# Second expert layer of two steps put together behind every even step of the first layer (steps 2 to 28)

## The reference

```python
h = x @ Wm + bm
t = h.reshape(bs * L_ * H, HD)              # 8 heads of 32 per token
logits = t @ expert_emb
w = jax.nn.softmax(logits, axis=-1)
topw, topi = jax.lax.top_k(w, K)            # K = 2 of 16 experts
hmid = jax.nn.gelu(jnp.einsum('td,edi->tei', t, W1) + b1, approximate=False)
eo = jnp.einsum('tei,eio->teo', hmid, W2) + b2
sel = jnp.take_along_axis(eo, topi[:, :, None], axis=1)
comb = (sel * topw[:, :, None]).sum(axis=1)
out = comb.reshape(bs, L_, d) @ Wo + bo
```

## Time and profile before

| | us |
|---|---|
| time, median of 3 runs | 3078.34 |
| lowest and highest | 3070.01, 3086.05 |
| the profiled execution, its own time | 3081.99 |
| its span, first to last instruction | 3080.3 |
| TensorE busy | 2900.5 |
| VectorE busy | 1912.2 |
| ScalarE busy | 1801.5 |
| GpSimd busy | 1326.3 |

### The profile page before, as it was taken

How to read it: one execution, slowest core, us unless ns; L and a number is a source line. 1 busy time by engine, 2 the same in 40 slices (tenths; PEclk the granted TensorE clock), 3 DMA queues, 4 the chain that set the end, 5 groups by cost and what they waited for, 6 DMA issues and landing times.

```text
span 3080.3 us, 51536 instructions
## 1 busy us (share of the span) xinstructions
PE 2900.5 (94%) x16460; PEld 1262.3 (41%) x16460; DVE 1912.2 (62%) x4637; ACT 1801.5 (58%) x2146; POOL 1326.3 (43%) x1355
## 2 busy tenths in 40 slices
PE   5689999999998999989999999999999999999999
PEld 2234444444444444444444444444444444444433
DVE  5465656757657566675666756666666657667453
ACT  1244675456754667546674466745676556754586
POOL 3312465135552365513644146542465225652254
PEclk7789999999999999999999999999999999999999
DMA  6101453024530344303442044420453113530242
GB/s 143 37 25 27 122 135 89 26 59 108 137 92 3 87 110 127 73 1 100 114 117 67 1 119 113 108 57 16 126 128 92 38 48 107 141 82 20 66 127 89
DMA packets 176245, 252.54 MB, mean 82 GB/s; under 512 B 50797, under 2 KB 82557, under 8 KB 175885
## 3 DMA queue, kind: packets, MB, share of 16 engines
q1 hardware_dynamic: 168988, 247.26, 31.0%
q10 hardware_dynamic: 6996, 1.99, 0.3%
HBM read 159.13 MB, written 12.63 MB: 56 GB/s over the span
## 4 chain that ended last, share of the span: by engine, by line
PE 84%; DVE 8%; issue 3%; ACT 1%; SPq 1%; DMA 0%; POOL 0%; POOLq 0%; ACTq 0%; DVEq 0%
PE ps L1248 17%; PE ps L1211 16%; PE ps L1266 16%; PE ps L1232 8%; PE ps L412 7%; PE ps L458 4%; PE ps L510 2%; PE ps L499 2%; PE ps L529 2%; PE ps L460 2%; DVE front L555 2%; PE ps L486 1%; PE ps L517 1%; PE ps L444 1%; PE ps L468 1%
## 5 line engine op out<-in xcount | busy, mean ns | idle before, releaser
L1330 ACT ACTIVATE rest<-ps 128x1024 f32<-128x1024 f32 x1024 | 993.1, 1022 | 372.8 <-PE ps L1248 370.2
L1312 ACT ACTIVATE rest<-ps 128x1024 f32<-128x1024 f32 (+3 forms) x768 | 607.4, 811 | 686.4 <-PE ps L1211 675.2
L1417 POOL TENSOR_TENSOR rest<-rest 128x512 f32<-128x512 f32 x480 | 630.6, 1314 | 654.2 <-DVE rest L1366 647.7
L552 DVE CUSTOM_DVE_ANT_0 rest<-ps,maskd 128x128 f32<-128x128 f32 (+3 forms) x1024 | 461.0, 488 | 283.9 <-PE ps L412 277.3
L1248 PE MATMUL ps<-wide,w1s 98*128 98x512 f32 x2048 | 624.5, 425 | 10.8 <-ACT rest L1330 10.8
L1407 POOL TENSOR_SCALAR_AFFINE_SELECT rest<-rest 128x256 f32<-128x256 f32 x512 | 216.6, 432 | 901.5 <-ACT rest L1312 875.6
L1266 PE MATMUL ps<-rest,w2s 128*32 128x512 f32 x4096 | 548.2, 607 | 0.6 <-ACT rest L1330 0.6
L1366 DVE SCALAR_TENSOR_TENSOR rest<-ps,b2c,wide 128x512 f32<-128x512 f32 x512 | 382.7, 747 | 266.0 <-PE ps L1266 240.5
L1248 PEld LDWEIGHTS ps<-wide,w1s 98*128 98x128 f32 x2048 | 339.3, 188 | 495.3 <-ACT rest L1330 355.4
L1211 PE MATMUL ps<-wide 49*128 49x512 f32 (+3 forms) x2304 | 498.6, 526 | 2.9 <-DMA wide<-front 2.9
L555 DVE TENSOR_REDUCE front<-ps 128x1 f32<-128x512 f32 x512 | 329.6, 685 | 163.6 <-PE ps L412 157.6
(11 more groups left out here) (136 smaller groups left out, 2328.6 us busy)
## 6 DMA issues: line engine op xcount, KB each, us to landing
wide<-gate_rows SPq DMA_DIRECT2D x1024, 128.0 KB, 2.8
wide<-front SPq DMA_DIRECT2D x480, 64.0 KB, 2.0
wide<-front SPq DMA_DIRECT2D x192, 128.0 KB, 2.3
ao<-in_x SPq DMA_DIRECT2D x16, 512.0 KB, 5.3
heads<-front SPq DMA_DIRECT2D x64, 128.0 KB, 2.4
xs<-in_x SPq DMA_DIRECT2D x16, 512.0 KB, 4.7
out<-xs SPq DMA_DIRECT2D x16, 512.0 KB, 3.5
wide<-ao SPq DMA_DIRECT2D x96, 64.0 KB, 2.3
```

The costliest lines, as they stand in the source:

```text
L552: v.tensor_tensor_reduce(out=R.junk[hh][:, 0:w], in0=src[:, 0:w], in1=L.maskd[:, HALF - w:], scale=1.0, scalar=-3e38, op0=ALU.add, op1=ALU ...
L1312: nc.scalar.activation(L.pt[:, u % PTS, :, f:HALF], L.ps[:, 2 * (u % 2):2 * (u % 2) + 2, 0:HALF - f], ACT.Exp, scale=SCALE).then_inc(S["c_ ...
L1330: nc.scalar.activation(L.hm[:, u % HM, :], bank(2 * (u % 2), 2), ACT.Gelu).then_inc(S["e_gelu"], 1)
L1417: g.tensor_tensor(dst, dst, L.gy[:, k % GY, :], ALU.add).then_inc(S["e_add"], 1)
```

## The change

For q from 2 to 28 the two outers `outer(q - 2)` and `outer(q - 1)` stand one behind the other in each even step, behind `inner(2q + 1)` and in front of the items of step q. Odd steps up to 27 have no outer, and step 1 has none. From step 29 on the order is the old one. VectorE follows in the same order: `gated(q - 2)` and `gated(q - 1)` in front of the items of an even step. ScalarE, GpSimd and SP keep their programs, and so do all the waits.

```diff
+TWOS = 28
...
+def outers_behind(q):
+
+
+    return (q - 2, q - 1) if 0 < q <= TWOS and q % 2 == 0 else ()
...
                     if q == 0:
                         values(img, NM - 1)
+                    for done in outers_behind(q):
+                        outer(img, done)
                     for item in eslots[img][q]:
                         item_matmuls(pe, L, RE[img], item)
-                    if q:
+                    if q > TWOS:
                         outer(img, q - 1)
...
                 for q in range(NQ):
+                    for done in outers_behind(q):
+                        gated(done)
                     for item in eslots[img][q]:
                         item_vector(v, L, RE[img], item)
-                    if q:
+                    if q > TWOS:
                         gated(q - 1)
```

## The result

The changed kernel took 3109.3 us in the median of 8 runs (3094.31 to 3118.77), the kernel before 3080.94 (3070.01 to 3094.46): ratio 1.0087, interval 1.0063 to 1.0111. Compared again later it was 1.0063 (1.0040 to 1.0086). So it is slower by 0.6 to 0.9%, on the side of 0.5% that the prediction held a little more likely, and by more than the 3092 it gave. Its upper end was 3108: the median lies just beyond, and by the ratio on the 3078.3 from which the prediction counted the time is 3105. The profiled execution took 3114.32 us, its span is 3112.6, 32.3 more than before.

A forecast was written before the change was run, and what follows sets the result against it. TensorE, busy 94% of the span, was taken as the bound. Images 0 to 6 -1.0, image 7 +12.6 and new clock falls 2.6 made 14 us: 3092 us against the median 3078.3, own range 3082 to 3096, 8 in 10 3079 to 3108.

The forecast's parts named there:

- The price of a pair without items: Two steps without items take 5.63 us against 4.43, +1.20 per pair, as the gelu waits for its buffer's outer.
- Steps 1 to 9: Images 0 to 6: step 1 to step 9 takes 25.36 us against 22.43, +2.9.
- clock term: Three new falls of TensorE's clock in all, 2.6 us; bounds 0 and fifteen falls, 13 us.
- the recurrence: Step starts worked out from which gelu or outer each instruction waits for; 5.63 us per pair without items.
- Steps 9 to 15: Idle before L510 shrinks from 1.47 to 0.35, no fall; step 15 0.6 earlier in images 0 to 4, 1.0 later in 5, 6.
- Steps 15 to 29: Images 0 to 6: 51.05 us against 51.03, switches saved and short waits before steps 19, 23 and 26 cancelling.
- The saving at the switches: Inner following a full-array item avoids switch costs; bounds 0 and 0.3 us per pair, taken near 0.3.
- rival 3: Slower: item then inner saves nothing, some 20 switches in 7 images lose 0.1 each; 8 us more, 3100 us; 22%.
- the sum of images 0 to 6: Change up to step 29: five images 0.6 us earlier, two 1.0 later, together -1.0 us.
- Image 7: Last image, without items to hide late gelus: +12.6 us up to step 29, reaching 94 us.
- rival 2: Slower: late gelus chop TensorE's work, ten to fifteen clock falls at 0.87 instead of three; 3102 us; 23%.
- Rival 1: Faster: the switches decide, each of 112 pairs saving 0.3, 34 us, with gelu lateness absorbed in images 0 to 6; 3049 us; 7%.

The follow-up runs named there:

- the run with six buffers: The changed kernel with six instead of four gelu buffers in the last image; one time, 3072.5 us.
- the repeats: Score matmuls of two attention slots repeated with the same operands: on the kernel before 3061.31 us (0.9934), on the changed kernel 3076.07 us (0.9988).
- second profile: The changed kernel again with no edit; median 3101.8 us, ratio 1.0063 to the kernel before.

## Why the prediction was right on the side and short on the size

**The price of a pair without items**: 5.63 worked out, 5.70 measured. The wait from the outer's start to the gelu was 1.20, not 1.13: `gated` started 1.14 behind the same outer, ScalarE ran one instruction of its wait first. The time of the step was right, its reason only partly: I laid the price on the buffer of the gelu, and the run with six buffers shows that most of it would be there without.

**Steps 1 to 9**: step 9 at 27.7 forecast, 27.75 found, step by step within 0.3 (8.55, 15.95, 22.08 for steps 3, 5, 7 against the 8.61, 16.21, 22.10 of the recurrence). In images 3 to 5 the clock fell once in these steps, +0.6: the "new falls" of the clock term. The prediction took image 6 for one without a fall, like image 5. It had no fall in step 10, but one in step 1 (105.81 us in all), and the changed kernel had one in step 2 of it (106.40).

**Steps 9 to 15**: right in kind. The idle time in front of L510 is gone altogether (0.35 forecast), the fall of the clock with it. L449 began 0.1 earlier and not 0.4 later (49.97 for 50.08 behind step 0), without the 1.59 of idle time that it had in front of it. Step 15 began 1.6 earlier than before in images 0 to 4, where I had 0.6; 0.3 of this is only that the record puts the first matmul of an inner earlier when it follows a full-array item (the second comes 0.64 behind it and not 0.34).

**Steps 15 to 29**: 51.87 for 51.03 against my 51.05 (51.57 without that 0.3). These two errors cancel: step 29 began at 105.13, forecast 105.3, and that it came so near is luck. The saving at the switches was taken rightly near its upper bound: the last matmul of L510 starts at 720.20 and the second of the inner behind it at 720.87, 0.43 + 0.24, so a full-array item then inner costs nothing, and rival 3 falls. The rule of the Trainium skill, "TensorEngine Tiling (Array Packing)", section Key Properties, that a change of the tiling mode drains TensorE, is borne out for the changes from or to the four column tiles of an outer, and the inner behind an item of 64 rows or 64 columns (`v`, `kc`, `std`) pays the 0.34 too; between a full-array item and an inner there is no such change, and no cost. Outer then full-array item costs 0.52 to the item's start, as I had carried over, but its first matmul of 512 columns takes 0.53 and not 0.43 (0.65 and 0.51 in front of L510), about 0.1 more in a pair.

**Steps 29 to 62**: here a term was left out. I closed the sum of images 0 to 6 at the *start* of step 29. The gelus of step 28 are late there, so step 29 takes 2.83 for 2.37 and nothing behind it gives the 0.47 back: 3.3 us over seven images, of the 3.6 of all eight. In image 7 I had counted it (0.3).

**Image 7**: +12.6 forecast, +13.7 found in the first profile, and +15.7 between the two kernels with the repeats (94.23 for 78.50), of which the slower has lower clock in two places and the faster in none. The mechanism was right: steps 17 to 28 took 36.7, which is the 34.2 of the sum and 2.5 for two falls. The table loads were nearly right: steps 15 and 16 took 10.2 for 8.6, 1.6 more where I had 1.3, with TensorE idle 3.55 in front of step 16 (the first line below) for 2.55. That the total is so near is luck again, as two things which the sum didn't hold nearly cancel. The kernel before had a fall in step 1 of this image (4.61 us for 3.04, the first window below), the changed one had not: step 9 began 1.4 later and not 2.9. And the changed one had the two falls, in the pairs without items at steps 20 and 28 (the other two windows, 5.05 and 5.12 for 3.85).

```profile
2976.54 2.14 PE L1255 MATMUL ps<-wide,w1s 98*128 98x512 f32 x4 [3.55 <-ACT rest L1339]
```
```profile
2906.91:2911.52 4.61, 4.43 (x17) 1.70 (x17) 0.68 (x2) 3.18 (x4) 0.50 (x1) 0.63 1.01 231
```
```profile
2989.08:2994.13 5.05, 4.87 (x21) 1.22 (x21) 2.86 (x5) 1.95 (x3) 1.84 (x2) 0.66 0.36 104
3013.07:3018.19 5.12, 4.92 (x20) 1.30 (x21) 0.75 (x1) 1.94 (x3) 0.86 (x2) 0.67 0.30 86
```

**The clock**: three new falls at 0.87 in the expert stages. Found in the first profile: one in steps 1 and 2 of each of images 3, 4 and 5, and two in image 7, against five gone at step 10 and one in step 1 of image 7. With 3 x 0.6 and 2 x 1.2 this is 4.2 for my 2.6, inside the bounds of the term, and rival 2 (ten to fifteen) falls. Pieces of 0.2 us rarely did it, but they did: in the pair of steps ahead of both falls of image 7 TensorE idled only 0.18 to 0.34 at a time. What the term missed is the attention stage. I had read its spread only as the 16 us between three runs and left it at "about what can't be told from no change". It is a cost that the kernel before carries in a certain amount, 3.7 us in five of seven stages and 2.4 in one, and that can double or vanish with no edit in those stages: 10.7 more in the first profile, 1.3 less in the second, 29 more with pairs from step 10 on. Of the 27 us that the ratio of the first comparison stands for, 15 to 17 are the order; the rest is this, the opening and the spread of the runs, which the record doesn't part.

**Rival 1**, that the switches decide, falls. Where the clock does not fall, steps 0 to 28 take 104.25 in the old order, 102.6 with all pairs from step 10 on and 102.9 with those at 10, 14 and 16 alone. Those three, where an outer moves ahead of an item that stalls, give 1.35 of the 1.65; the other seven pairs, which save switches, give 0.3 together.

## What to carry to other kernels

Grouping like matmuls saves a few tenths of a us per switch, but each group starves the engine that is fed by the other kind; count how many inputs lie ready for it before the group starts, not only the buffers behind it. A piece of work pays when it is moved in front of an instruction that stalls, so move it there and nowhere else: of the fourteen pairs of an image three gave nearly all there was to gain. And when TensorE has idle places of 1.5 us and more anywhere in the kernel, close them before other changes are judged, since the lower clock behind them can give back a gain of 0.5% as a loss of the same size.

## What the runs showed of the hardware

The same attention stage, by its instructions, took about 174.1, 176.5, 177.8, 179.4, 180.9 and 182.1 us, with 0, 7, 10, 14, 17 and 20 us of lower clock in it. Behind an idle place of 1.7 or 2.4 us the clock sometimes fell and sometimes not, with equal work in front of it. Within one execution the same value tended to come back image after image: counted from step 0 of one image to that of the next, four in a row of 372.02 to 372.05 us in the kernel before, and four of 368.62 to 368.68 in the changed one's second profile. With pairs from step 10 on the images took 372.3, 373.5 or 373.8: steps 0 to 28 shorter by 3.3 us (1.7 with a fall in step 1) than in those images of 372.05, and images no shorter. That the moment of the idle place decides, so that a kernel can settle on a good or a bad value, would fit this; it is argued, not shown, as no run moved the idle place alone. Doing the second score block before such a place three or four times took 2.4 us of TensorE's time per image, and the stage came to 174.1 in place of 177.8.

A matmul that is repeated with the same operands before it is signalled kept the clock up: no fall in the 35 attention stages of the five kernels with the repeats. The profile of the kernel with six buffers, without repeats, had none there either, in seven images of 368.6 to 368.7 us, so one profile without falls proves little.

The clock also fell behind much shorter idle pieces. In step 1 of image 7 of the kernel before it fell behind 0.82 and 0.18 us, in steps 20 and 28 of image 7 of the changed kernel, where each inner waits for a gelu, behind pieces of 0.18 to 0.34 us.
